# A Mamba-2 block and a gated Hadamard FFN on one core: broadcast loads, sums of squares and raw loads of the first sample put in other places

## The reference

```python
z, xBC, dt = split(xn @ w_in)                  # 1024 | 1280 | 16 columns
dt  = softplus(dt + dt_bias)
xBC = silu(conv4(xBC) + conv_b)                # causal, depthwise
X, B, C = split(xBC)                           # 16 heads x 64 | 128 | 128
y = ssd(X * dt, dt * -exp(A_log), B, C) + X * D
y = y * silu(z)
mamba = (y * rsqrt(mean(y * y) + EPS) * norm_w) @ w_out
hidden = fwht(silu(xn @ W1.T) * (xn @ W3.T))   # 2048 wide
ffn = hidden @ W2.T
```

## Time and profile before

| | |
|---|---|
| median of 3 runs | 997.19 us |
| the profiled execution | 999.73 us |
| its span (first to last instruction) | 997.9 us |
| mean granted TensorE clock | 0.977 of full speed |
| PE busy | 947.4 us, 95% |
| DVE, ACT, POOL busy | 579.8, 352.2, 323.6 us |
| POOL idle until the broadcast sums land (L1431) | 278.8 us in 16 times |
| broadcast of cs_rows, issue to landing | 5.9 us (median of 16) |

### The profile page before, as it was taken

The page is one execution under the profiler, slowest core; times in us unless marked ns, Lnnn a source line. Parts: engine busy times, 40 slices in busy tenths (PEclk is TensorE's granted clock), DMA queues, the critical chain, the costliest instruction groups (busy, mean ns, idle before and its releaser), DMA issues.

```text
span 997.9 us, 13278 instructions
## 1 busy us (share of the span) xinstructions
PE 947.4 (95%) x4999; PEld 473.0 (47%) x5000; DVE 579.8 (58%) x959; ACT 352.2 (35%) x544; POOL 323.6 (32%) x362
## 2 busy tenths in 40 slices
PE   8799858887999999999999999999999999999997
PEld 4344434443534444555545445554545445555543
DVE  7876567667453576655652576666551766665521
ACT  5587745423232333331221333332221344232200
POOL 2000524474200021863610202855510202855410
PEclk9999898888999999999999999999999999999999
DMA  9578452615431433544322434454322535255122
GB/s 335 198 239 305 168 160 73 211 45 177 137 106 64 172 102 109 179 139 120 113 85 64 162 105 137 138 159 118 115 64 64 172 105 153 73 156 148 43 75 94
DMA packets 76206, 134.25 MB, mean 135 GB/s; under 512 B 7536, under 2 KB 20464, under 8 KB 74096
## 3 DMA queue, kind: packets, MB, share of 16 engines
q1 hardware_dynamic: 56640, 104.88, 33.7%
q10 hardware_dynamic: 19504, 28.53, 9.2%
HBM read 107.43 MB, written 25.95 MB: 134 GB/s over the span
## 4 chain that ended last, share of the span: by engine, by line
PE 78%; DVE 9%; ACT 3%; POOL 3%; issue 3%; DMA 3%; ACTq 0%; DVEq 0%; SPq 0%; POOLq 0%
PE ps L594 51%; PE ps L831 15%; PE ps L792 2%; PE ps L784 2%; PE ps L778 2%; DMA arena<-cs_rows 2%; DVE arena L1227 2%; PE ps L718 1%; PE ps L747 1%; DVE arena L1173 1%; PE ps L764 1%; ACT arena L997 1%; POOL arena L1431 1%; ACT arena L917 1%; DMA arena<-w 1%
## 5 line engine op out<-in xcount | busy, mean ns | idle before, releaser
L594 PE MATMUL ps<-xh,arena 128*128 128x512 f16 x1592 | 492.7, 383 | 6.6 <-DVE arena L1173 6.6
L594 PE MATMUL ps<-xl,arena 128*128 128x512 f16 x796 | 304.7, 383 | 0.0
L594 PEld LDWEIGHTS ps<-xh,arena 128*128 128x128 f16 x1592 | 159.6, 100 | 196.9 <-issue 11.7
L831 PE MATMUL ps<-arena 128*128 128x512 f16 x768 | 171.1, 379 | 0.0
L1421 POOL TENSOR_TENSOR arena<-arena 128x512 f16<-128x512 f32 x64 | 78.7, 1234 | 237.5 <-ACT arena L967 237.5
L1431 POOL TENSOR_TENSOR arena<-arena 128x2048 f32<-128x2048 f32 x16 | 58.1, 3634 | 278.8 <-DMA arena<-cs_rows 278.8
L594 PEld LDWEIGHTS ps<-xl,arena 128*128 128x128 f16 x796 | 78.4, 99 | 90.3 <-issue 6.1
L831 PEld LDWEIGHTS ps<-arena 128*128 128x128 f16 x768 | 74.3, 98 | 91.0 <-issue 5.5
L1227 DVE SCALAR_TENSOR_TENSOR arena<-ps,cw,arena 128x511 f32<-128x511 f32 (+2 forms) x120 | 89.5, 748 | 45.6 <-ACT arena L957 43.7
L967 ACT ACTIVATE arena<-arena 128x512 f16<-128x512 f32 x64 | 40.3, 630 | 185.5 <-DVE arena L1248 185.5
L594 PE MATMUL ps<-wo_hi,arena 128*128 128x512 f16 x256 | 80.8, 388 | 0.2 <-DVE arena L1370 0.2
(11 more groups left out here) (182 smaller groups left out, 1094.3 us busy)
## 6 DMA issues: line engine op xcount, KB each, us to landing
arena<-w_parts SPq DMA_DIRECT2D x198, 256.0 KB, 2.7
w_parts<-arena SPq DMA_DIRECT2D x66, 256.0 KB, 3.0
arena<-cs_rows ACTq DMA_DIRECT2D x16, 1024.0 KB, 5.9
arena<-w SPq DMA_DIRECT2D x24, 512.0 KB, 4.8
arena<-ecs_rows ACTq DMA_DIRECT2D x24, 256.0 KB, 6.6
arena<-x ACTq DMA_DIRECT2D x18, 256.0 KB, 3.6
w_mid<-arena SPq DMA_DIRECT2D x8, 512.0 KB, 3.1
arena<-w_mid SPq DMA_DIRECT2D x16, 256.0 KB, 2.7
```

The source lines that it names most:

```text
L594: ins = nc.tensor.matmul(out_ap, lhs(i, a), rhs(i, c), start=(i == 0 and s == 0), stop=(i == n - 1 and s == 2))
L831: ins = nc.tensor.matmul(bank(t), hw[a][:, i, t * P:(t + 1) * P], w2s[i % W2R][:, d, :], start=(i == 0 and s == 0), stop=(i == JF - 1 and ...
```

## The change

It gives the broadcast load of `csbc` for c > 0 a step of its own, L, that stands 5 or 6 tiles (sample 0) or 3 to 5 tiles (the others) ahead of E; E keeps the two loads of `ecsb`. It splits the sum of quads 3 and 4 into two, so that there are eight QS; the waits on `scale_13` follow from that. In sample 0 it moves SQ, QS, WOQ, WOS, WOH, XL, W, N, V and ROW by some tiles. It changes which quad takes which space in the buffer (quad 5 the space that quad 6 had, and the other way round) and when it is loaded. WOQ stands at one per tile from n = 2 on.

```diff
-QUAD_SUMS = ((0,), (1,), (2,), (3, 4), (5,), (6,), (7,))
-QUADS_EARLY = 4
+QUADS_EARLY = 3
-FIRST_AT = ([("WOL", 0, 1)] + [("WOQ", q, q // 2 + 4) for q in range(8)] + [("WOS", 0, 9)] +
-            [("WOH", q, at) for q, at in enumerate((10, 10, 11, 11, 12, 13, 14, 15))] +
-            [("SQ", 2, 1), ("QS", 2, 3), ("SQ", 3, 4), ("SQ", 4, 5), ("QS", 3, 7), ("SQ", 5, 12), ("QS", 4, 13), ("SQ", 6, 15),
-             ("QS", 5, 18), ("SQ", 7, 19), ("QS", 6, 20)] +
-            [("XL", 0, 17), ("HL", 0, 28), ("W2S", 0, 25)] +
+FIRST_AT = ([("WOL", 0, 1)] + [("WOQ", q, q + 2) for q in range(8)] + [("WOS", 0, 11)] +
+            [("WOH", q, at) for q, at in enumerate((12, 12, 13, 14, 14, 15, 16, 17))] +
+            [("SQ", 2, 1), ("QS", 2, 3), ("SQ", 3, 6), ("QS", 3, 8), ("SQ", 4, 9), ("QS", 4, 11), ("SQ", 5, 12), ("QS", 5, 13),
+             ("SQ", 6, 16), ("QS", 6, 17), ("SQ", 7, 20), ("QS", 7, 21)] +
+            [("XL", 0, 18), ("HL", 0, 28), ("W2S", 0, 25)] +
...
-STEP_FIRST = {"T": (4, 12, 20, 29), "X": (6, 15, 23, 32), "S": (7, 15, 23, 33), "R": (9, 18, 26, 35), "E": (None, 10, 18, 26),
-              "Y": (9, 17, 25, 34), "N": (12, 19, 27, 36), "Q": (12, 19, 27, 36), "V": (14, 21, 29, 38), "W": (16, 23, 30, 40),
-              "ROW": (15, 22, 30, 39)}
+STEP_FIRST = {"T": (4, 12, 20, 29), "X": (6, 15, 23, 32), "S": (7, 15, 23, 33), "R": (9, 18, 26, 35), "L": (None, 5, 12, 20),
+              "E": (None, 10, 18, 26), "Y": (9, 17, 25, 34), "N": (12, 20, 27, 36), "Q": (12, 20, 27, 36), "V": (14, 22, 29, 38),
+              "W": (18, 24, 30, 40), "ROW": (15, 23, 30, 39)}
...
 STEP_AT = {
...
+    "L": (None, 3, 9, 17),
     "E": (None, 6, 14, 22),
...
-    for place, load in ((13, (4, 0)), (15, (4, 1)), (20, (6, 0)), (27, (5, 0)), (28, (5, 1)), (30, (6, 1)), (33, (7, 0)), (34, (7, 1))):
+    for place, load in ((13, (4, 0)), (15, (4, 1)), (20, (5, 0)), (28, (5, 1)), (30, (6, 0)), (32, (6, 1)), (35, (7, 0)), (36, (7, 1))):
...
+            if quad == 5:
+                return raw_pair if kind == 0 else hid_raw[:, :, 5]
             if quad == 6:
-                return raw_pair if kind == 0 else hid_raw[:, :, 7]
-            first = 5 if quad == 5 else 2 * quad
-            return hid_raw[:, kind, first:first + 2]
+                return hid_raw[:, :, 6 + kind]
+            return hid_raw[:, kind, 2 * quad:2 * quad + 2]
...
             elif quad == 5:
-                sp.wait_ge(w_lo.sem, w_lo.at(0, quad_tile(3, kind, 0)))
+                sp.wait_ge(w_lo.sem, w_lo.at(0, 1 if kind == 0 else quad_tile(2, 1, 1)))
             elif quad == 6:
-                sp.wait_ge(w_lo.sem, w_lo.at(0, 1 if kind == 0 else quad_tile(3, 1, 1)))
+                sp.wait_ge(w_lo.sem, w_lo.at(0, quad_tile(3, 1, kind)))
...
-                        elif i in (4, 6):
-                            pe.wait_ge(yscl_ok.sem, yscl_ok.at(0, (i - 4) // 2))
                         elif i == 5:
-                            pe.wait_ge(mamba_evac.sem, mamba_evac.at(0, 0))
-                        pe.wait_ge(sq_quads, 2 * (QUAD_SUMS[i][-1] + 1))
+                            pe.wait_ge(yscl_ok.sem, yscl_ok.at(0, 0))
+                        elif i == 6:
+                            pe.wait_ge(mean_read.sem, mean_read.at(0, 0))
+                        elif i == 7:
+                            pe.wait_ge(yscl_ok.sem, yscl_ok.at(0, 1))
+                        pe.wait_ge(sq_quads, 2 * (i + 1))
...
                     elif kind == "WOS":
-                        pe.wait_ge(scale_13, 4)
+                        pe.wait_ge(scale_13, 5)
...
                             pe.wait_ge(mamba_evac.sem, mamba_evac.at(b, c - 1))
-                            if b == 0 and c == 1:
-                                pe.wait_ge(scale_13, 6)
...
                         if b == 0 and c < 2:
-                            pe.wait_ge(scale_13, 5 + 2 * c)
+                            pe.wait_ge(scale_13, 6 + 2 * c)
...
                             pe.wait_ge(wo_l, QE)
+                            pe.wait_ge(scale_13, 7)
...
-                    elif kind == "E":
+                    elif kind == "L" or (kind == "E" and c == 0):
...
                         act.wait_ge(esub_ok.sem, esub_ok.at(b, c - 1))
                         act.dma_start(csbc.rearrange("p h l -> p (h l)"),
                                       cs_rows[b, c].rearrange("h l -> (h l)").partition_broadcast(P)).then_inc(d_csbc, 16)
-                        if c > 0:
-                            act.wait_ge(t1_ok.sem, t1_ok.at(b, c - 2))
-                            for r in range(2):
-                                act.dma_start(ecsb[HD * r:HD * r + HD, :].rearrange("p (q l) -> p q l", q=QE),
+                    elif kind == "E":
+                        act.wait_ge(d_cst, (b + 1) * 32)
+                        act.wait_ge(t1_ok.sem, t1_ok.at(b, c - 2))
+                        for r in range(2):
+                            act.dma_start(ecsb[HD * r:HD * r + HD, :].rearrange("p (q l) -> p q l", q=QE),
```

More of the change, by code:

```diff
@@ L36 @@
 QUADS = 2 * JF // 4
-QUAD_SUMS = ((0,), (1,), (2,), (3, 4), (5,), (6,), (7,))
-QUADS_EARLY = 4
-SUMS_OF = {q: n for n, quads in enumerate(QUAD_SUMS) for q in quads}
+QUADS_EARLY = 3
 G1_ACT, G1_POOL, G1_DVE = 2, 2, 3
@@ L727, in _ @@
                             pe.wait_ge(sq_w2_dve, JF // 4)
[L728 to L729 removed]
                         elif i == 5:
[L731 to L733 removed]
+                            pe.wait_ge(yscl_ok.sem, yscl_ok.at(0, 0))
[4 more added lines that the diff above has]
+                        pe.wait_ge(sq_quads, 2 * (i + 1))
                         to = bank(FREE_BANK)
[L735 to L736 removed]
+                        nc.tensor.matmul(to[:, 2:4], ones, row_sq[:, SQ_Q + 2 * i:SQ_Q + 2 * i + 2], start=True, stop=False)
+                        ins = nc.tensor.matmul(to[:, 2:4], ones, row_sq[:, SQ_FREE:SQ_FREE + 2], start=False, stop=True)
                         if i == 3:
@@ L911, in split_hi @@
                 else:
-                    act.wait_ge(scale_13, SUMS_OF[(p - N_FRONT) // 4] + 1)
+                    act.wait_ge(scale_13, (p - N_FRONT) // 4 + 1)
                 act.wait_ge(tile_done.sem, tile_done.at(0, p - PARTS))
@@ L1145, in to_scale @@
             def to_scale(n, sums, op):
-                k = steps.step(nc.vector.tensor_reduce(out=total[:, n:n + 1], in_=sums, axis=AX.X, op=op))
+                v, h = total[:, n:n + 1], half[:, n:n + 1]
+                k = steps.step(nc.vector.tensor_reduce(out=v, in_=sums, axis=AX.X, op=op))
                 dve.wait_ge(steps.sem, k)
-                scale_of(n, 1, total[:, n:n + 1])
-            def scale_of(n, m, v):
-                h = half[:, n:n + m]
                 k = steps.step(nc.vector.tensor_scalar(h.bitcast(I32), v.bitcast(I32), 1, 0x3F800000, ALU.logical_shift_right,
@@ L1155, in scale_of @@
                 dve.wait_ge(steps.sem, k)
-                steps.step(nc.vector.tensor_scalar(scl[:, n:n + m].bitcast(I32), h.bitcast(I32), -1, 204 << 23, ALU.mult, ALU.add))
-                k = steps.step(nc.vector.tensor_scalar(inv[:, n:n + m].bitcast(I32), h.bitcast(I32), 1, 50 << 23, ALU.mult, ALU.add))
+                steps.step(nc.vector.tensor_scalar(scl[:, n:n + 1].bitcast(I32), h.bitcast(I32), -1, 204 << 23, ALU.mult, ALU.add))
+                k = steps.step(nc.vector.tensor_scalar(inv[:, n:n + 1].bitcast(I32), h.bitcast(I32), 1, 50 << 23, ALU.mult, ALU.add))
                 dve.wait_ge(steps.sem, k)
@@ L1279, in _ @@
                         dve.wait_ge(quad_sums, i + 1)
-                        lo, n = W13 + QUAD_SUMS[i][0], len(QUAD_SUMS[i])
+                        n = W13 + i
                         if i == 3:
                             to_scale(W2, bank(FREE_BANK)[:, 8:17], ALU.add)
-                        k = steps.step(nc.vector.tensor_reduce(out=total[:, lo:lo + n], axis=AX.X, op=ALU.max,
-                                                               in_=bank(FREE_BANK)[:, 2:2 + 2 * n].rearrange("p (q k) -> p q k", k=2)))
-                        dve.wait_ge(steps.sem, k)
-                        scale_of(lo, n, total[:, lo:lo + n])
-                        nc.vector.tensor_scalar(f_13[:, lo - W13:lo - W13 + n], inv[:, lo:lo + n], 0.5 / XS, None,
-                                                ALU.mult).then_inc(scale_13, 1)
+                        to_scale(n, bank(FREE_BANK)[:, 2:4], ALU.max)
+                        nc.vector.tensor_scalar(f_13[:, i:i + 1], inv[:, n:n + 1], 0.5 / XS, None, ALU.mult).then_inc(scale_13, 1)
                     elif kind == "W2S":
```

2 lines of the change are left out of this document (1 added, 1 removed).

## The result

The changed kernel takes 1007.12 us (median of 4 runs, 1005.86 to 1008.43), the kernel before 997.78 (4 runs, 996.74 to 998.92) beside it: a ratio of 1.0093, 95% interval 1.0073 to 1.0114. It is 9.3 us slower, where 991.7 was forecast. The profiled execution took 1008.43.

A forecast was written before the change was run, and what follows sets the result against it. PE's own work bounds samples 1 to 3; sample 0 had 30.0 us idle and 14.5 of low clock. These fall to 26.9 and 12.8: 4.8, plus 0.7 in sample 2, 5.5 less, giving 991.7 us; range 984.5 to 1002.

The forecast's parts named there:

- part 4: Broadcast asked for at L: S2's 2.7 us idle and 3.1 low clock go in sample 0; samples 1 to 3 gain 0.72.
- the 0.72 us: PE's only missing busy time in the 20 us windows from 340 to 980 us, counted as gained in sample 2.
- The sign that the prediction itself gave for being wrong: Any of: no wait at WOS, a wait of ACT at L, or idle PE beyond 340 us.
- Rival (d): Slower: the subtraction ahead of DVE reaches PE in chunks 2 and 3 of sample 0 too, 1003.1 us; chance 0.22.
- Part 1: WOQ moved up, sample 0: ACT waits 6.1 us for w_out, PE idles 5.6 against 4.9 us; roughly nothing.
- Part 2: Own sum per quad, WOS behind QS4, sample 0: the 12.9 us wait becomes 10.6 at WOS plus 3.2 at QS5.
- Part 3: W0 two tiles later, QS6 earlier, sample 0: QS6 waits some 2.3 us (bounds 0 and 5), N1's 4.3 us goes.
- the 5.8 us booked for S2: Part 4's gain in sample 0, chunk 2: 2.7 us of idle and 3.1 us of low clock at S2 go.
- Rival (b): The change does what it is drawn for, quad 5's transfer being the limit: 22.8 us less, 974 us; chance 0.08.
- Rival (c): The new waits give back the gain: QS6 takes 5 us and a 2.6 slow stretch, 995.7 to 997; chance 0.20.

The follow-up runs named there:

- the one with the gate first: The changed kernel, all early loads kept, with GpSimd's subtraction in samples 1 to 3 also waiting for the gate of the chunk before: 996.12 us, ratio 0.9965.
- the buffer alone: The kernel before, with only quads 5 and 6 swapping spaces in the buffer and loaded at the new places: 996.52 us, ratio 0.9968.
- the kernel it was made from: The changed kernel with the gate ahead of the subtraction, WOQ at its old places and chunk 1's subtraction in sample 0 behind split 31: 991.60 us, ratio 0.9926.

## Why the prediction was wrong

**The step that failed** is in part 4: "In samples 1 to 3 nine subtractions start about 3 us sooner and meet the gate (L1348, two SBUF inputs) of the chunk before, 2.4 us late; bank by bank the next eviction still comes 2 us before PE wants it. There I count the 0.72 us as gained." The meeting was seen, and its size about right (nine gates held, three by 2.3 us and six by 2.7). What was followed from there was the wrong thread: the banks that DVE empties, and not ACT's square of the gated product, for which N waits. That path had no slack to give 2.7 us: before, the square's sum was out at 437.24 and N ran at 438.58, 1.3 us of room, and a gate 2.7 us longer uses it and 1.3 more. The result is 1.26 us of idle six times. With 0.28 at L765 that makes 2.8 of the 3.7 us a sample that the changed kernel takes over the one with the gate first; the last section comes to the rest. The sentence that samples 1 to 3 are PE's own work and that no shift of a load helps there was nearly true of gains. It was read as if it held for losses too. The sign that the prediction itself gave for being wrong, idle PE beyond 340 us, is the one that came.

**The sign.** Rival (d) named the right mechanism, the lock reaching PE, and the right ending, but put it into chunks 2 and 3 of sample 0. In chunk 2 it does hold two splits (2.8 and 2.0 us, at 192 and 196), and PE's waits there are 0.5 and 1.5 us; the loss was elsewhere. The range ended at 1002, and 1007 lay outside. The Trainium skill, SBUF — State Buffer, section Who interferes with whom, has the rule that decides this case: the pair of ports is one exclusive lock, and who issues first keeps it. The runs agree, 1.28 us when the gate goes first and 4.01 when it doesn't. The prediction used the rule at tile 31 and at the gate. At tile 31 it followed the held operation to PE; at the gate, which is held nine times, it followed only one of the paths behind it. The second split in chunk 2, at 195.79, is held by GpSimd's clip (1.89 us from 195.39), as rival (d) also thought possible.

**Part 1** was right in kind: ACT's wait of 6.49 us for w_out (6.1 forecast), PE idle 3.2 at that place (2.4 forecast), then 1.0 and 0.9 (2.9 for both). "Roughly nothing" was a cost of 2.2 us: the sum compared idle times only and took the slow stretch as unchanged, and with WOQ at its old places both the idle and the slow stretch are smaller.

**Part 2** was right nearly to the tenth: WOS at 144.72 (144.8), idle 11.0 (10.6), split 31 of 3.63 us, A5 at 143.30 (143.7), QS5 at 157.87 (157.8) after 3.6 (3.2). The run with split 31 first puts the lock's share at 2.9 us of idle and about 2 us of time.

**Part 3**: QS6 idle 3.4 us (2.3), and a stretch at the lower clock behind it, counted at half; N1's idle is gone, as said, but V1 waits 1.5 us for the next quad's scale, which was not in the sum.

**Part 4, sample 0**: S2's wait is gone, as forecast. But its worth was read from one execution, and the order that made it was a matter of 0.3 us. The kernel with only the early load of samples 1 to 3 has sample 0's old order, and its profile shows no wait at S2 and reaches the first long piece of the chain at 329.55, where the kernel before had 333.48. At 193 us the two are 0.7 us apart; where they part is chunk 2's subtraction. In the kernel before, the low-half split is first:

```profile
194.60 0.75 DVE L1173 SCALAR_TENSOR_TENSOR arena<-arena,scl 128x512 f16<-128x512 f32 x1 [0.61 <-ACT arena L917]
194.88 3.94 POOL L1431 TENSOR_TENSOR arena<-arena 128x2048 f32<-128x2048 f32 x1 [5.77 <-DMA arena<-cs_rows]
```

In the other the subtraction is first:

```profile
193.67 3.61 POOL L1433 TENSOR_TENSOR arena<-arena 128x2048 f32<-128x2048 f32 x1 [5.05 <-DMA arena<-cs_rows]
194.15 3.68 DVE L1175 SCALAR_TENSOR_TENSOR arena<-arena,scl 128x512 f16<-128x512 f32 x1 [0.58 <-ACT arena L918]
```

There the held split delays the scale for which V1 waits: PE stands 2.2 us at V1 instead of 2.7 at S2, and S2 runs at 208.01 (207.63 before). What is gone is the slow stretch of 6.8 us behind S2, 3.1 us of time by the prediction's reckoning; in its place there is one of 3.4 us behind V1. Two more profiles, of the buffer alone and of L at E's places in all samples, also show a wait at V1 (2.2 and 2.3 us) and none at S2. So 3.9 us of sample 0 differ between two executions of the same order, and of the 5.8 us booked for S2 the idle part only moves. The profiled execution was 2.5 us above its median, which the prediction noted and did not follow up.

The idle of sample 0 was forecast at 26.9 and the rows of the changed kernel give 29.6; the loss to the clock 12.8 and 12.9. Before, it was 30.9 counted in the same way (the 30.0 of the prediction leaves out 0.75 at V2 and 0.22 behind H0) and 14.5. That would be a gain of 2.9 us in the rows, of which 1.6 are seen at the long piece (331.86 against 333.48). The three profiles with the changed order and early loads in sample 0 reach it at 331.2 to 331.9, the two with the whole old order at 333.5 and 329.6: the same in the mean. By the times of the kernel with late loads in samples 1 to 3 it is 0.1 us, with an interval from 1.4 faster to 2.7 slower.

**Rival (b)**, the transfer of quad 5 as the true limit, falls: the buffer alone gives 3 us, and not 20, and with the transfer moved and split 31 ahead of the lock, PE still stands 8.1 us at WOS and 3.6 at QS5. Some of the 3 may be the same scatter as S2's; its interval leaves out zero, but which wait gave it stays open. **Rival (c)** had the size of sample 0 about right, by luck: QS6 took 3.4 us and not its 5, and WOQ's 2.2 us, which it did not name, were part of what gave the gain back.

## What to carry to other kernels

When a load is moved forward, ask what its lateness was ordering. A GpSimd instruction that waited for data ran behind a VectorE instruction by accident; with the data there it runs in front and holds it for its whole length. State the wanted order with a wait of its own, which cost nothing here and turned 1007.1 into 996.1 us. And follow a delayed instruction to everyone who reads its output, first of all in the stretches that repeat: 1.3 us twice a sample outweighed all that sample 0 could give.

## What the runs showed of the hardware that was not expected

A VectorE operation with one input was held as well. In the kernel with QS6 later, the scaling of a 128 x 512 tile, whose shortest took 0.54 us in the same run, met the subtraction:

```profile
181.40 3.92 DVE L1374 TENSOR_SCALAR arena<-arena 128x512 f32<-128x512 f32 x1
181.43 3.61 POOL L1429 TENSOR_TENSOR arena<-arena 128x2048 f32<-128x2048 f32 x1
```

The prediction took operations of one SBUF input as free of the lock, and left out the condition that goes with it: the Trainium skill, SBUF — State Buffer, section Who interferes with whom, excepts those that may run in a mode of two ports, a tensor_scalar among them. The row agrees. It even starts 0.03 us before GpSimd's, so the order of two starts this close in the trace does not tell who holds the ports.

The lock also holds the other way: in the rows of the kernel before at 194.60, GpSimd's subtraction started 0.28 us behind VectorE's split and took 3.94 us, where most take 3.61.

A stall of PE cost more than its idle row: six waits of 1.26 us and three of 0.28 make 8.4, and the three samples took 11.1 us longer than with the gate first (224.6, 224.6 and 225.3 against 220.9, 220.9 and 221.6). Part of it is how the rows are drawn. One of PE's matmuls of the changed kernel just before the first of these waits:

```profile
436.70 0.38 PE L594 MATMUL ps<-xl,arena 128*128 128x512 f16 x1
```

The next one starts at 436.92, 0.22 us on, while each is drawn 0.38 long, as they overlap. An idle time is counted from the drawn end, and so leaves out 0.16 us of each stall: nine times 0.16 is 1.4 of the missing 2.7 us. Most of the other 1.3 shows when the matmuls of the two kernels are set side by side. The two small matmuls of N are drawn 0.38 us behind a wait and 0.28 without one (L804 in the rows of the two kernels above), 0.1 us six times. And V0 (L809, at 410.66) starts 0.17 us late in each sample, too little for a row of idle: the gate of chunk 0, held 3.57 us, delays the reduction for which V0 waits. That leaves 0.2 us.

Two waits close together can share one slow stretch. In the kernel with WOS later, one stretch at 1.2 GHz covers the waits of both WOS and N0, where the kernel it was made from had one behind WOS and another behind QS5. PE is busy at 1.2 GHz for 16.3 us of sample 0 from 100 us on, and 20.0 in the other kernel; half of the difference, 1.8 us, is an estimate of what that gives of the 3.9 us by which sample 0 ends sooner (322.11 against 326.04). A window of the shared stretch:

```profile
138.70:148.70 10.00, 7.92 (x26) 4.80 (x27) 9.83 (x17) 4.63 (x8) 9.64 (x6) 0.50 0.64 224
```
